# Mixture-of-experts stage on one core: weight fetches in two transfers and shorter runs, with the third, fourth and second expert and the last tiles placed anew

## The chip, the cores and the metric

One core of a Trainium2 chip runs the whole program. The metric is the device time in microseconds of one execution, so less is better. Times below are from one execution under the hardware profiler, counted from the start of its span, unless a median of runs is named.

## What is computed

Four residual blocks over x of 4 x 1024 rows of 256 channels, each behind a layer norm:

```python
x = x + attn0(layernorm(x))       # 16 heads, circulant projections
x = x + moe(layernorm(x))         # the stage that the change touches
x = x + attn1(layernorm(x))       # 16 heads with a position bias, gated output
x = x + ffn1(layernorm(x))        # 256 x 256 on fp8-rounded rows

# moe: 8 experts, top 2 of each row by a Sinkhorn plan pi, D = 256, F = 1024
g = jnp.einsum('nd,efd->enf', xf, W_gate)
u = jnp.einsum('nd,efd->enf', xf, W_up)
y = jnp.einsum('enf,edf->end', jax.nn.silu(g) * u, W_down)
out = out + y[top_idx[:, k], n_ar] * pi[:, k:k + 1]       # k = 0, 1
```

Everything is float32 at the surface. The kernel splits each float32 operand of a product into a rounded "high" part and the rest, "low", and adds three products (high x high, high x low, low x high).

## The kernel before, in words

The experts' stage (class Experts) runs from about 719 to 1453 us of the profile. The 8192 pairs of row and expert are sorted by expert into 71 tiles of 128 rows (MOE_TILES); the tiles of one expert follow one another, about nine each. `plan` is a small table in SBUF, filled at run time, which says for every tile which expert it belongs to, which experts come next (SECOND, THIRD, FOURTH), whether the tile is the first of a new expert (IS_NEW), and which of the two weight buffers it uses (BUFFER, OTHER_BUFFER). Whoever needs such a number reads it with `planned` (L2351: a load and two register instructions).

An expert's weights are 3 MB: gate, up and down, 8 KB each per partition. They are kept three times, as they came (e_w_raw) and as high and low parts (e_w_high, e_w_low), each with two buffers. ACT makes the high parts (`high_part`, `high_second`), DVE the low ones (`low_part`, `low_second`); `high_ready` and `low_ready` count the parts in a fixed order over the tiles, and a part is counted, by a drain, in tiles without a new expert too. When both are made of a raw buffer, it is free for the fetch of the expert after next but one.

For each tile j, on the engines:

- PE (`pe`): gate product, transposes of the next tile's rows, up product, then the down product of tile j-2 (LAG = 2). A gate and up product are 24 matmuls, a down product 24 shorter ones.
- ACT (`act`): `split_hidden(j-2)` (high part of the turned hidden rows, e_hT), SiLU of the gate product (e_hid), the conditional fetch of an expert (`fetch_fourth(j-2)`), `high_part` of gate and up, `move_y(j-2)` (e_y from PSUM), `high_part` of down.
- DVE (`dve`): `rest_of_hidden(j-2)` (low part of e_hT), `low_part` of down and of up, `split_rows(j+1)` (e_xT), the product of SiLU and up (e_hid), its 32 x 32 transposes (e_squares), `low_part` of gate.
- SP (`sync`): stores e_squares to DRAM (`store_squares`, 512 KB) and loads them back turned (`load_turned`, four transfers, runs of 1 KB). The last two tiles (BY_PE and on) are turned by PE instead (`turn_hidden`).
- POOL: gathers the rows of a tile, scatters its results.

The order is written out by hand; nothing schedules it. The first expert comes by SP in three transfers ahead of the stage; the second and the third (L2385) by SP too, right behind each other; the fourth by POOL, once `low_second` has released the second's raw buffer, which is in tile 1, 2 or 3 if the expert changes there and otherwise behind tile 3 (REST = 4). All later fetches are ACT's, 3 MB in one transfer in runs of 4 KB (WEIGHT_RUN), in the second tile after a change of expert; `cond` makes them no transfer in all other tiles. At a change, tile s, the next expert's gate and up are made high in tile s of ACT, its down in tile s+1, and low one after the other in DVE's tiles s, s+1 and s+2.

Of the kernel before, what the change touches and what calls it, by code (L numbers as in the profile page):

```python
# [2069 lines left out]
W_BUFS = 2  # L2070
WEIGHT_RUN = 4096
AHEAD = W_BUFS + 1
# [239 lines left out]
class Experts:  # L2312
# [3 lines left out]
    BY_PE = MOE_TILES - LAG  # L2316
    REST = 4
    Q, R = 4, 32
# [34 lines left out]
    def high_value(self, kind, j):  # L2353


        order = []
        for k in range(1, MOE_TILES):
            order += [("second", k)] * (k < self.REST) + [("up", k)] + [("down", k - 1)] * (k > 1)
            order += [("second", k + 1)] * (k + 1 == self.REST)
        return order.index((kind, j)) + 1  # L2360

    def low_value(self, kind, j):


        order = []
        for k in range(1, MOE_TILES):
            order += [("second", k)] * (k < self.REST) + [("down", k - self.LAG)] * (k > self.LAG)
            order += [("up", k - 1)] * (k > 1) + [("gate", k)]
            order += [("second", k + 1)] * (k + 1 == self.REST)
        order += [("up", MOE_TILES - 1), ("down", MOE_TILES - 2)]  # L2370
        return order.index((kind, j)) + 1
# [12 lines left out]
    def fetch(self, e, buf, row, j, sem):  # L2384
        e.dma_start(self.w.raw[:, buf, :],  # L2385
                    self.w.weights[bass.ds(self.planned(e, row, j), 1), :, :].rearrange("e p n -> p (e n)")
                    ).then_inc(sem, DMA)

    def sync(self, e, mirror_stored, beside):
        e.wait_ge(self.rows_in[1], DMA)  # L2390
        mirror_stored(e)
        self.fetch(e, 0, SECOND, 0, self.second_in)
        e.wait_ge(self.first_low, 3)
        beside(e, (2, 3))
        self.fetch(e, 1, THIRD, 0, self.weights_in)
        for j in range(self.BY_PE):
            self.store_squares(e, j)
            self.load_turned(e, j)
        e.wait_ge(self.second_in, DMA)
# [36 lines left out]
    def pool(self, e):  # L2436
        def fetch_fourth(k):
            with self.if_second(e, k):
                e.wait_ge(self.low_ready, self.low_value("second", k))
                self.fetch(e, 0, FOURTH, 0, self.fourth_in)  # L2440

        e.wait_ge(self.routed, 1)
        for j in range(ROW_BUFS):
            self.load_rows(e, j)
        e.wait_ge(self.routed, 2)
        for j in range(MOE_TILES):
            if 1 <= j < self.REST:
                fetch_fourth(j)
# [4 lines left out]
            if j + 1 == self.REST:  # L2453
                fetch_fourth(self.REST)
        for j in range(MOE_TILES - self.LAG, MOE_TILES):
            self.store_y(e, j)
        e.wait_ge(self.fourth_in, DMA)
        for o in range(Y_BUFS):
            e.wait_ge(self.y_out[o], DMA * ((MOE_TILES + Y_BUFS - 1 - o) // Y_BUFS))

    def act(self, e):
# [8 lines left out]

        def high_part(j, a, b):
            with e.If(self.planned(e, IS_NEW, j) > 0):
                e.wait_ge(self.weights_in, DMA * min(max(1, j - 1), MOE_TILES - 1 - self.LAG))
                if j >= 2:
                    e.wait_ge(self.fourth_in, DMA)
                high_of(bass.ds(self.planned(e, OTHER_BUFFER, j), 1), a, b)
            e.drain().then_inc(self.high_ready, 1)

        def fetch_fourth(j):
            e.wait_ge(self.low_ready, self.low_value("down", j))  # L2480
            e.dma_start(self.w.raw[:, bass.ds(self.planned(e, OTHER_BUFFER, j), 1), :],
                        self.w.weights[bass.ds(self.planned(e, FOURTH, j), 1), :, :].rearrange("e p n -> p e n"),
                        cond=self.planned(e, IS_NEW, j) > 0, max_dma_last_dim=WEIGHT_RUN).then_inc(self.weights_in, DMA)

# [7 lines left out]
        def split_hidden(j):  # L2492
            self.wait_turned(e, j)
            if j:
                e.wait_ge(self.downed, j)
            high, whole = self.parts_of_hidden(j, 0)
            e.activation(high, whole, ACT.Copy).then_inc(self.h_high, 1)  # L2497

        for j in range(MOE_TILES):
# [9 lines left out]
            e.activation(self.hid[:, :], self.GU[:, 0, :], ACT.Silu).then_inc(self.silu, 1)  # L2509
            if self.LAG < j < MOE_TILES - 1:  # L2510
                fetch_fourth(j - self.LAG)
            if j >= 1:
                e.wait_ge(self.upped, j)
                high_part(j, 0, DOWN_AT)
            if j >= self.LAG:
                move_y(j - self.LAG)
                high_part(j - 1, DOWN_AT, WIDE)
            if j + 1 == self.REST:
                high_second(self.REST)
        for j in range(self.BY_PE, MOE_TILES):  # L2520
            split_hidden(j)
            move_y(j)

    def wait_turned(self, e, j):
        if j < self.BY_PE:
            e.wait_ge(self.turned_in[j % 2], self.Q * DMA * (j // 2 + 1))
        else:
            e.wait_ge(self.h_turned, j - self.BY_PE + 1)

    def parts_of_hidden(self, j, part):  # L2530

        out = self.hT[:, part, :, :].bitcast(FP32R)
        if j >= self.BY_PE:
# [5 lines left out]
    def dve(self, e, beside):  # L2539
# [10 lines left out]
        def rest_of_hidden(j):  # L2550
            low, whole = self.parts_of_hidden(j, 1)
            high = self.hT[:, 0, :, :]
# [3 lines left out]
            if j:  # L2556
                e.wait_ge(self.downed, j)
            e.tensor_tensor(low, whole, high, ALU.subtract).then_inc(self.h_low, 1)  # L2558
# [44 lines left out]
        for j in range(MOE_TILES):  # L2603
# [13 lines left out]
            if j:  # L2617
# [5 lines left out]
        low_part(MOE_TILES - 1, "up", DC * F, DOWN_AT)  # L2623
        low_part(MOE_TILES - 2, "down", DOWN_AT, WIDE)
        for j in range(self.BY_PE, MOE_TILES):
            rest_of_hidden(j)

    def pe(self, e):
# [60 lines left out]
        def down(j):  # L2689
# [7 lines left out]
            for f in range(FC):  # L2697
                mm = product(j, self.Y, (self.hT[:, 0, f, :], self.hT[:, 1, f, :]), DOWN_AT + f * D, D, f == 0,
                             f == FC - 1)
# [4 lines left out]
        for j in range(MOE_TILES):  # L2704
# [736 lines left out]
```

## Time and profile before

| | |
|---|---|
| median of 3 runs | 2167.04 us (2166.58 to 2167.49) |
| profiled execution, its own time | 2164.73 us |
| its span | 2163.1 us |
| mean granted TensorE clock | 0.937 of full |
| experts' stage | 719 to 1453 us |
| busy in the span: PE, DVE, ACT, POOL | 89%, 62%, 64%, 33% |

A row of the timeline gives start and duration in us, engine, line, operation and tiles, and in brackets the idle time before it with what ended that. "issue" is time with no wait that the profile shows. ACTq, SPq and DVEq are the sequencers' own instructions. The chain of waits is followed back from the last instruction of the span or of a window. Of the DMA views, q1 is SP's queue, q10 is ACT's and q0 is POOL's.

### The profile page before, as it was taken

To read this page: it belongs to the slowest core of one execution; us is meant where nothing else is said; L and a number is where in the kernel's file an instruction comes from. 1 tells how busy PE (TensorE), PEld (TensorE's weight loads), DVE (VectorE), ACT (ScalarE), POOL (GpSimd) and SP (SyncE) were. 2 spreads that over 40 slices of the span, in tenths; PEclk is the share of its full clock that TensorE was granted. 3 is DMA by queue.
4 is the path that set the end of the run, shared out by engine and by line. 5 is a ranking of instruction groups with operands and counts; after the bars stand their busy time and mean duration, and the time that the engine had idled before them with its cause. 6 is when DMAs were issued, how large, how long until landed. Compare 5 with 4: busy or idle time off the path is not lost.

```text
span 2163.1 us, 37845 instructions
## 1 busy us (share of the span) xinstructions
PE 1915.4 (89%) x11671; PEld 1090.0 (50%) x11671; DVE 1331.6 (62%) x2221; ACT 1385.9 (64%) x1586; POOL 703.1 (33%) x697
## 2 busy tenths in 40 slices
PE   6999999999945579998998989976989999999998
PEld 5722333333332468887887878865722222222255
DVE  4511144445667545555465555427689999999967
ACT  5699999999832233233233233224799999999944
POOL 2000111111110212121222122111068888888932
PEclk9999999999955689999999999987999999999999
DMA  5744333444100644554544554529944426354021
GB/s 195 243 97 69 59 77 76 83 88 88 40 31 17 246 161 144 200 180 143 199 167 154 191 186 140 187 91 333 315 106 90 103 43 133 59 139 67 9 87 69
DMA packets 131072, 276.08 MB, mean 128 GB/s; under 512 B 18588, under 2 KB 69022, under 8 KB 129656
## 3 DMA queue, kind: packets, MB, share of 16 engines
q1 hardware_dynamic: 117160, 228.72, 38.2%
q10 hardware_dynamic: 6736, 22.94, 3.1%
q0 software_dynamic: 6960, 21.77, 3.0%
q8 instruction: 108, 1.77, 0.4%
q14 instruction: 108, 0.88, 0.1%
HBM read 365.58 MB, written 96.21 MB: 213 GB/s over the span
## 4 chain that ended last, share of the span: by engine, by line
PE 46%; ACT 21%; DVE 13%; DMA 7%; issue 7%; POOL 3%; DVEq 1%; ACTq 1%; SPq 1%; POOLq 0%
PE psum L2654 16%; PE psum L1345 12%; PE psum L1326 9%; ACT A1f_probs L1370 8%; ACT A1f_probs L1378 8%; DMA hidden<-e_squares 4%; PE psum L381 3%; DVE e_w_low L2575 2%; ACT e_w_high L2463 2%; DMA e_turned<-hidden 2%; POOL A1f_probs L1547 2%; PE psum L850 1%; DVE e_hT L2558 1%; PE psum L396 1%; ACTq L2351 1%
## 5 line engine op out<-in xcount | busy, mean ns | idle before, releaser
L1326 PE MATMUL psum<-A_qa,A_ka 50*128 50x512 f32 x2048 | 408.3, 467 | 23.5 <-DVE A_qa L1413 6.2
L1326 PEld LDWEIGHTS psum<-A_qa,A_ka 50*128 50x128 f32 x2048 | 176.4, 185 | 470.5 <-DVE A1f_probs L1423 243.4
L2654 PE MATMUL psum<-e_w_high,e_xT 128*128 x1136 | 389.5, 406 | 22.0 <-DVE e_xT L2548 20.2
L1547 POOL TENSOR_TENSOR A1f_probs<-A1f_probs,A1f_bias 128x512 f32<-128x512 f32 x256 | 327.1, 1288 | 81.4 <-ACT A1f_probs L1378 81.0
L1423 DVE SCALAR_TENSOR_TENSOR A1f_probs<-psum,A1f_bias 128x1024 f32<-128x1024 f32 x256 | 311.6, 1217 | 23.5 <-PE psum L1326 19.7
L1378 ACT ACTIVATE A0f_probs<-psum 128x1024 f32<-128x1024 f32 x256 | 315.5, 1232 | 0.0
L1366 ACT ACTIVATE A0f_probs<-psum 128x1024 f32<-128x1024 f32 x256 | 313.2, 1224 | 2.7 <-PE psum L1326 2.7
L2654 PE MATMUL psum<-e_w_high,e_hT 128*128 x1136 | 236.8, 301 | 59.6 <-DVE e_hT L2558 59.6
L1345 PE MATMUL psum<-A1f_probs,v 128*32 128x512 f32 x2048 | 274.0, 606 | 17.2 <-POOL A1f_probs L1547 16.2
L1370 ACT ACTIVATE A1f_probs<-A1f_probs 128x1024 f32<-128x1024 f32 x256 | 274.0, 1070 | 4.5 <-DVE A1f_probs L1423 3.5
L1345 PE MATMUL psum<-A0f_probs,v 128*32 128x512 f32 x2048 | 273.8, 607 | 0.0
L1378 ACT ACTIVATE A1f_probs<-psum 128x1024 f32<-128x1024 f32 x256 | 263.7, 1030 | 0.0
L2654 PEld LDWEIGHTS psum<-e_w_high,e_xT 128*128 128x128 f32 x1136 | 219.2, 193 | 67.9 <-issue 24.4
L2433 POOL DMA_INDIRECT results<-e_y,places x71 | 70.4, 992 | 549.0 <-ACT e_y L2490 539.3
L2490 ACT ACTIVATE e_y<-psum 128x256 f32<-128x256 f32 x71 | 27.2, 384 | 323.5 <-PE psum L2654 322.4
L2654 PEld LDWEIGHTS psum<-e_w_high,e_hT 128*128 128x128 f32 x1136 | 197.9, 208 | 69.5 <-issue 67.5
L2654 PE MATMUL psum<-e_w_low,e_xT 128*128 x568 | 225.8, 397 | 0.0
L2558 DVE TENSOR_TENSOR e_hT<-e_turned,e_hT 128x1024 fp32r<-128x1024 f32 x69 | 86.0, 1247 | 149.1 <-ACT e_hT L2497 145.2
L2654 PE MATMUL psum<-e_w_low,e_hT 128*128 x568 | 170.0, 299 | 0.0
L2497 ACT ACTIVATE e_hT<-e_turned 128x1024 fp32r<-128x1024 f32 x69 | 73.1, 1060 | 95.5 <-DMA e_turned<-hidden 65.9
L1431 DVE SCALAR_TENSOR_TENSOR psum<-A1f_bias,psum 128x512 f32<-128x512 f32 x195 | 133.5, 685 | 0.0
L2654 PEld LDWEIGHTS psum<-e_w_low,e_xT 128*128 128x128 f32 x568 | 110.5, 195 | 18.6
(297 smaller groups left out, 2506.3 us busy)
## 6 DMA issues: line engine op xcount, KB each, us to landing
e_w_raw<-in_experts ACTq DMA_DIRECT2D x67, 3072.0 KB
hidden<-e_squares SPq DMA_DIRECT2D x69, 512.0 KB
e_turned<-hidden SPq DMA_DIRECT2D x276, 128.0 KB
qk_parts<-L_part SPq DMA_DIRECT2D x64, 512.0 KB, 4.1
A_qa<-qk_parts SPq DMA_DIRECT2D x192, 128.0 KB, 4.2
A_ka<-qk_parts SPq DMA_DIRECT2D x192, 128.0 KB, 6.3
om<-results SPq DMA_DIRECT2D x16, 512.0 KB, 6.9
e_w_raw<-in_experts SPq DMA_DIRECT2D x2, 3072.0 KB
```

What stands on the lines that cost most here:

```text
L1326: mm = e.matmul(ps[:, side * HALF:(side + 1) * HALF], self.qk.ka[rows, s, pair, kt * P:(kt + 1) * P].bitcast(FP32R), self.qk.qa[rows, s, p ...
L1345: pv = e.matmul(O[32 * i:32 * (i + 1), :], self.v[:, b * BT + kt, h * VW:h * VW + 32], self.probs_of(n, i // PAIR)[:, side * HALF:(side + ...
L1366: e.activation(probs, self.buffer(w), ACT.Exp, scale=SCORE_SCALE).then_inc(self.exped[0], 1)
L1370: e.activation(probs, probs, ACT.Exp).then_inc(self.exped[0], 1)
L1378: e.activation(self.probs_of(n, 1), self.buffer(w), ACT.Exp, scale=SCORE_SCALE).then_inc(self.exped[1], 1)
L1423: e.scalar_tensor_tensor(out=self.probs_of(n, 0).rearrange("p (h q) -> p h q", h=PAIR), in0=self.buffer(w).rearrange("p (h q) -> p h q", h ...
L1431: e.scalar_tensor_tensor(out=third, in0=self.bias_of(*w[1:], slice(PAIR, PAIR + 1)).rearrange("p h q -> p (h q)"), scalar=1.0 / SCORE_SCAL ...
L1547: e.tensor_tensor(fourth, fourth, self.bias_of(*w[1:], slice(self.FOURTH, GH)).rearrange("p h q -> p (h q)"), ALU.mult).then_inc(self.mult ...
L2433: e.indirect_dma_start(out=self.y_dram, out_offset=bass.IndirectOffsetOnAxis(ap=self.places[:, j:j + 1], axis=0), in_=self.y[:, o, :], in_ ...
L2497: e.activation(high, whole, ACT.Copy).then_inc(self.h_high, 1)
L2558: e.tensor_tensor(low, whole, high, ALU.subtract).then_inc(self.h_low, 1)
L2654: mm = e.matmul(out, left[part].bitcast(FP32R), moving.bitcast(FP32R), start=start and i == 0, stop=stop and i == 2)
```

## The change

It does five things.

1. Every fetch but the first expert's goes in runs of 1 KB (WEIGHT_RUN).
2. ACT's fetch becomes two: gate and up (2 MB) one tile after the new expert's first (`fetch_part(j-1, "up")`), down (1 MB) two tiles after (`fetch_part(j-2, "down")`). Each waits until its own part has been made low. Both stand in every tile, as transfers that `cond` may leave out. The first is where the SiLU's side of `move_y` is, the second behind the down part's `high_part`.
3. The third expert is fetched by ACT, behind the SiLU of tile 0, and the fourth by ACT behind the SiLU of tile 2; POOL has no fetch left.
4. REST goes from 4 to 2: `high_second` and `low_second` run behind tile 1.
5. The last tiles: tile 69's turned rows are kept in the two buffers of e_turned, free by then, and split ahead of the work of tile 70; PE turns tile 70 ahead of the down product of 69. SP's first loads of the next stage, which reuse that space, wait until that product is done. Parts that only a change at the last tile would need are left out.

```diff
-WEIGHT_RUN = 4096
+WEIGHT_RUN = 1024
...
-    REST = 4
+    REST = 2
+    LAST = MOE_TILES - 1
...
     def sync(self, e, mirror_stored, beside):
...
         beside(e, (2, 3))
-        self.fetch(e, 1, THIRD, 0, self.weights_in)
...
-        e.wait_ge(self.h_low, self.BY_PE)
+        e.wait_ge(self.downed, self.BY_PE + 1)
...
-        def fetch_fourth(j):
-            e.wait_ge(self.low_ready, self.low_value("down", j))
+        def fetch_part(j, kind, a, b, landed):
+            e.wait_ge(self.low_ready, self.low_value(kind, j))
...
             e.activation(self.hid[:, :], self.GU[:, 0, :], ACT.Silu).then_inc(self.silu, 1)
-            if self.LAG < j < MOE_TILES - 1:
-                fetch_fourth(j - self.LAG)
-            if j >= 1:
+            if j == 0:
+                e.wait_ge(self.first_low, 3)
+                self.fetch(e, 1, THIRD, 0, self.weights_in)
+            if j == self.REST:
+                e.wait_ge(self.low_ready, self.low_value("second", self.REST))
+                self.fetch(e, 0, FOURTH, 0, self.fourth_in)
+            if 1 <= j < self.LAST:
                 e.wait_ge(self.upped, j)
-                high_part(j, 0, DOWN_AT)
+                high_part(j, "up", 0, DOWN_AT)
+            if 1 < j < self.LAST - 1:
+                fetch_part(j - 1, "up", 0, DOWN_AT, self.weights_in)
+            if j == self.LAST:
+                split_hidden(self.BY_PE)
             if j >= self.LAG:
                 move_y(j - self.LAG)
-                high_part(j - 1, DOWN_AT, WIDE)
+                high_part(j - 1, "down", DOWN_AT, WIDE)
+            if self.LAG < j < self.LAST:
+                fetch_part(j - self.LAG, "down", DOWN_AT, WIDE, self.second_in)
...
+            if j == self.LAST:
+                rest_of_hidden(self.BY_PE)
             multiply(j)
...
-        down(MOE_TILES - self.LAG)
-        turn_hidden(MOE_TILES - 1)
-        down(MOE_TILES - 1)
+        turn_hidden(self.LAST)
+        down(self.BY_PE)
+        down(self.LAST)
```

ACT between `move_y` (e_y) and the next `split_hidden` (e_hT), in any middle tile. Before, from the down part's `high_part` on:

```order
L2463 ACTIVATE e_w_high<-e_w_raw 128x2048
L2472 UNCONDITIONAL_BRANCH
L2497 ACTIVATE e_hT<-e_turned 128x4x8x32
L2509 ACTIVATE e_hid<-psum 128x1024
L2351 TENSOR_LOAD plan
```

The change, from the same instruction on:

```order
L2455 ACTIVATE e_w_high<-e_w_raw 128x2048
L2464 UNCONDITIONAL_BRANCH
L2352 TENSOR_LOAD plan
L2352 ISA x2
L2352 TENSOR_LOAD plan
L2352 ISA x2
L2352 TENSOR_LOAD plan
L2352 ISA x2
L2476 ISA x2
L2476 DMA e_w_raw<-in_experts 128x8x256
L2494 ACTIVATE e_hT<-e_turned 128x4x8x32
```

A fetch with its three readings of the plan now stands between the two, in every tile.

ACT in tile 70. Before, behind that tile's last high part:

```order
L2497 ACTIVATE e_hT<-psum 128x1024 [waits e_downed,e_h_turned]
L2490 ACTIVATE e_y<-psum 128x256 [waits e_y_out0,e_downed]
L2497 ACTIVATE e_hT<-psum 128x1024 [waits e_downed,e_h_turned]
L2490 ACTIVATE e_y<-psum 128x256 [waits e_y_out1,e_downed]
L3273 ACT_TABLE_LOAD [waits met]
```

The change, from the SiLU of tile 70 on:

```order
L2506 ACTIVATE e_hid<-psum 128x1024 [waits e_hidden,e_gated]
L2494 ACTIVATE e_turned<-psum 128x1024 [waits e_h_low,e_h_turned]
L2485 ACTIVATE e_y<-psum 128x256 [waits e_y_out2,e_downed]
...
L2494 ACTIVATE e_hT<-psum 128x1024 [waits e_downed,e_h_turned]
L2485 ACTIVATE e_y<-psum 128x256 [waits e_y_out0,e_downed]
L2485 ACTIVATE e_y<-psum 128x256 [waits e_y_out1,e_downed]
```

Tile 69's split has moved ahead of the e_y of tile 68 and no longer waits for a down product; only tile 70's does, for that of tile 68.

## Rows read from the trace of the kernel before

**Rows 1.** The page: busy time of each engine and its share of the span.
```profile
PE 1915.4 (89%) x11671; PEld 1090.0 (50%) x11671; DVE 1331.6 (62%) x2221; ACT 1385.9 (64%) x1586; POOL 703.1 (33%) x697
```

**Rows 2.** Chain of waits, start and length in us: the beginning, then two middle tiles.
```profile
731.81 16.18 DMA hidden<-e_squares
...
777.42 6.56 DVE e_w_low L2575
...
987.00 8.38 PE psum L2654 x48
995.60 8.39 PE psum L2654 x48
```

**Rows 3.** Timeline, PE: idle ahead of the down products of tiles 0 and 2.
```profile
755.19 0.58 PE L2654 MATMUL psum<-e_w_high,e_hT 128*128 x1 [14.63 <-DVE e_hT L2558]
...
785.53 0.58 PE L2654 MATMUL psum<-e_w_high,e_hT 128*128 x1 [9.60 <-DVE e_hT L2558]
```

**Rows 4.** Timeline, all engines, one middle tile.
```profile
931.18 0.38 ACT L2490 ACTIVATE e_y<-psum 128x256 f32<-128x256 f32 x1 [4.82 <-PE psum L2654]
...
932.02 1.06 ACT L2497 ACTIVATE e_hT<-e_turned 128x1024 fp32r<-128x1024 f32 x1 [0.46 <-issue]
...
933.12 1.26 DVE L2558 TENSOR_TENSOR e_hT<-e_turned,e_hT 128x1024 fp32r<-128x1024 f32 x1 [2.24 <-ACT e_hT L2497]
...
936.71 0.28 PE L2654 MATMUL psum<-e_w_high,e_hT 128*128 x1
```

**Rows 5.** Timeline, DVE, around the change of expert at 1175.
```profile
1170.77 1.27 DVE L2558 TENSOR_TENSOR e_hT<-e_turned,e_hT 128x1024 fp32r<-128x1024 f32 x1 [2.23 <-ACT e_hT L2497]
1173.15 0.42 DVE L2546 CAST e_xT<-psum 128x256 fp32r<-128x256 f32 x1 [1.11 <-issue]
...
1182.55 1.22 DVE L2558 TENSOR_TENSOR e_hT<-e_turned,e_hT 128x1024 fp32r<-128x1024 f32 x1 [0.19 <-issue]
1185.39 2.29 DVE L2575 TENSOR_TENSOR e_w_low<-e_w_raw,e_w_high  x1 [1.61 <-issue]
```

**Rows 6.** Timeline, ACT, around the same change.
```profile
1168.84 0.38 ACT L2490 ACTIVATE e_y<-psum 128x256 f32<-128x256 f32 x1 [4.84 <-PE psum L2654]
...
1175.60 3.63 ACT L2463 ACTIVATE e_w_high<-e_w_raw  x1 [2.98 <-issue]
...
1188.41 1.91 ACT L2463 ACTIVATE e_w_high<-e_w_raw  x1 [0.94 <-issue]
1190.48 1.06 ACT L2497 ACTIVATE e_hT<-e_turned 128x1024 fp32r<-128x1024 f32 x1 [0.15 <-issue]
...
1223.17 0.38 ACT L2490 ACTIVATE e_y<-psum 128x256 f32<-128x256 f32 x1 [6.01 <-PE psum L2654]
```

**Rows 7.** Timeline, SP: a store and the load behind it, with no fetch beside them.
```profile
1168.57 0.34 SPq L2409 DMA_DIRECT2D hidden<-e_squares  x1
1171.18 1.73 SPq L2419 DMA_DIRECT2D e_turned<-hidden  x4
```

**Rows 8.** Chain of waits: the store that goes beside a fetch.
```profile
1200.19 9.12 DMA hidden<-e_squares
```

**Rows 9.** DMA queues: q1 in 1172 to 1176 (1 KB runs), q10 in 1197 to 1212.
```profile
q1 hardware_dynamic: 576, 0.52, 41.8%
...
q10 hardware_dynamic: 784, 3.15, 60.2%
```

**Rows 10.** Timeline, ACT: e_y of tiles 5, 67 and 70.
```profile
818.29 0.38 ACT L2490 ACTIVATE e_y<-psum 128x256 f32<-128x256 f32 x1 [4.82 <-PE psum L2654]
...
1426.56 0.38 ACT L2490 ACTIVATE e_y<-psum 128x256 f32<-128x256 f32 x1 [4.84 <-PE psum L2654]
...
1452.84 0.38 ACT L2490 ACTIVATE e_y<-psum 128x256 f32<-128x256 f32 x1 [6.05 <-PE psum L2654]
```

**Rows 11.** Windows, 1216 to 1223: the granted clock is the third number from the end.
```profile
1216.00:1223.00 7.00, 5.35 (x25) 5.36 (x26) 4.45 (x5) 1.16 (x2) 0.00 (x0) 0.53 0.30 92
```

**Rows 12.** Timeline, PE: the down product of tile 69.
```profile
1439.06 0.58 PE L2654 MATMUL psum<-e_w_high,e_hT 128*128 x1 [3.29 <-DVE e_hT L2558]
```

More of the change, by code:

```diff
@@ L2357, in high_value @@
         for k in range(1, MOE_TILES):
-            order += [("second", k)] * (k < self.REST) + [("up", k)] + [("down", k - 1)] * (k > 1)
+            order += [("second", k)] * (k < self.REST) + [("up", k)] * (k < self.LAST)
+            order += [("down", k - 1)] * (k > 1)
             order += [("second", k + 1)] * (k + 1 == self.REST)
@@ L2367, in low_value @@
             order += [("second", k)] * (k < self.REST) + [("down", k - self.LAG)] * (k > self.LAG)
-            order += [("up", k - 1)] * (k > 1) + [("gate", k)]
+            order += [("up", k - 1)] * (k > 1) + [("gate", k)] * (k < self.LAST)
             order += [("second", k + 1)] * (k + 1 == self.REST)
-        order += [("up", MOE_TILES - 1), ("down", MOE_TILES - 2)]
+        order += [("down", self.LAST - 1)]
         return order.index((kind, j)) + 1
@@ L2436, in pool @@
     def pool(self, e):
[L2437 to L2440, printed above, removed]
         e.wait_ge(self.routed, 1)
@@ L2469, in high_second, with high_part @@
             e.drain().then_inc(self.high_ready, 1)
-        def high_part(j, a, b):
+        def high_part(j, kind, a, b):
             with e.If(self.planned(e, IS_NEW, j) > 0):
-                e.wait_ge(self.weights_in, DMA * min(max(1, j - 1), MOE_TILES - 1 - self.LAG))
-                if j >= 2:
-                    e.wait_ge(self.fourth_in, DMA)
+                if kind == "down":
+                    e.wait_ge(self.second_in, DMA * min(max(1, j - 1), MOE_TILES - 1 - self.LAG))
+                else:
+                    e.wait_ge(self.weights_in, DMA * min(max(1, j - 1), MOE_TILES - 1 - self.LAG))
+                    if j >= 2:
+                        e.wait_ge(self.fourth_in, DMA)
                 high_of(bass.ds(self.planned(e, OTHER_BUFFER, j), 1), a, b)
             e.drain().then_inc(self.high_ready, 1)
-        def fetch_fourth(j):
-            e.wait_ge(self.low_ready, self.low_value("down", j))
-            e.dma_start(self.w.raw[:, bass.ds(self.planned(e, OTHER_BUFFER, j), 1), :],
-                        self.w.weights[bass.ds(self.planned(e, FOURTH, j), 1), :, :].rearrange("e p n -> p e n"),
-                        cond=self.planned(e, IS_NEW, j) > 0, max_dma_last_dim=WEIGHT_RUN).then_inc(self.weights_in, DMA)
+        def fetch_part(j, kind, a, b, landed):
+            e.wait_ge(self.low_ready, self.low_value(kind, j))
+            e.dma_start(self.w.raw[:, bass.ds(self.planned(e, OTHER_BUFFER, j), 1), a:b],
+                        self.w.weights[bass.ds(self.planned(e, FOURTH, j), 1), :, a:b].rearrange("e p n -> p e n"),
+                        cond=self.planned(e, IS_NEW, j) > 0, max_dma_last_dim=WEIGHT_RUN).then_inc(landed, DMA)
         def move_y(j):
@@ L2528, in wait_turned, with hT_free, hT_of @@
             e.wait_ge(self.h_turned, j - self.BY_PE + 1)
+    def hT_free(self, j):
+        return self.BY_PE if j == self.LAST else j
+    def hT_of(self, j, part):
+        return self.turned[:, part, :].rearrange("p (f n) -> p f n", f=FC) if j == self.BY_PE else self.hT[:, part, :, :]
     def parts_of_hidden(self, j, part):
-        out = self.hT[:, part, :, :].bitcast(FP32R)
+        out = self.hT_of(j, part).bitcast(FP32R)
         if j >= self.BY_PE:
@@ L2551, in rest_of_hidden @@
             low, whole = self.parts_of_hidden(j, 1)
-            high = self.hT[:, 0, :, :]
+            high = self.hT_of(j, 0)
             high = high.rearrange("p f n -> p (f n)") if j >= self.BY_PE else high.rearrange(
@@ L2555, in rest_of_hidden @@
             e.wait_ge(self.h_high, j + 1)
-            if j:
-                e.wait_ge(self.downed, j)
+            if j and j != self.BY_PE:
+                e.wait_ge(self.downed, self.hT_free(j))
             e.tensor_tensor(low, whole, high, ALU.subtract).then_inc(self.h_low, 1)
@@ L2622, in dve @@
                 next(beside, None)
[L2623 to L2626, printed above, removed]
+        low_part(self.LAST - 1, "down", DOWN_AT, WIDE)
+        rest_of_hidden(self.LAST)
     def pe(self, e):
```

22 lines of the change are left out of this document (10 added, 12 removed).

## The prediction

> **What bounds the kernel now.** I read the page first: PE is busy for 89% of the span and no other engine for more than 64% [rows 1], so what isn't PE's work shows up as idle PE. In the chain of waits a middle tile takes 995.60 - 987.00 = 8.60 us, all of it PE [rows 2]; 71 tiles would be 611 us, and the stage takes some 734. Three places hold the rest.
>
> The beginning: PE idles 14.63 us before down product 0 and 9.60 before down product 2 [rows 3]. The first is the store of tile 0, which lands 16.18 us after its issue, behind the second and third expert on SP's queue; the second is the second expert's conversion, its low part alone 6.56 us, at a time when nothing else waits [rows 2].
>
> The seven changes of expert: from the e_y of tile 5 to that of tile 67 are 608.3 us [rows 10], 62 tiles at 8.60 are 533.2, so a change loses 10.7 us. At the one I followed, five tiles take 1223.17 - 1168.84 = 54.3 us, a loss of 11.3 [rows 6]. Half of that is order: DVE turns to e_hT only behind its low part [rows 5]. The other half is the DMA: a store lands in 2.6 us by itself [rows 7] and in 9.12 beside the fetch [rows 8]; PE then waits, and its clock is granted at 0.53 of full, so for nearly all of these 7 us at 1.2 GHz, the lower level [rows 11].
>
> The end: PE idles 3.29 us before down product 69 [rows 12], since e_hT is one buffer and each split waits for the product before.
>
> **The change, part by part.**
>
> *Beginning.* The third expert leaves SP's queue, so the store of tile 0 shares the engines with it in place of standing behind it. Ahead of it are the second expert and two 0.5 MB loads. It landed at 748.0 [rows 2]; by bytes (about 4.7 MB ahead and in turn with the third's) I take 743.5, between 740 (the third gets no share) and 748 (all bytes must go first). The second expert's high part (REST = 2) is made while PE waits for that store anyway. DVE then does its squares of tile 1 and the low part: some 2.2 us from the squares' start to the low part, 6.56 for it [rows 2], 1.24 for e_hT, so down product 0 starts at 753.8, 1.4 earlier. Then nothing is left to convert: tiles follow at PE's pace, down product 2 at 772.9 instead of 785.53 [rows 3]. The fourth expert's transfer (ACT at about 753) now falls on the store of tile 2, priced at 1.5 us. Behind that the old kernel still loses 2 us to its fourth fetch and 2 to the lower clock, until e_y of tile 5 at 818.29 [rows 10]. Together -15 us; bounds -17 and -9.
>
> The Trainium skill (DMA: Bandwidth & Descriptors, Issuing engines are not separate DMA queues) says that transfers of all issuers run on the same 16 engines and interleave, so that spreading them saves only issue time. By that rule the store still lands at 748, and this term is -11, not -15.
>
> *Every middle tile.* Between e_y and e_hT on ACT there are 0.84 us now (931.18 to 932.02) [rows 4]. One fetch costs ACT's sequencer 2.98 - 0.94 = 2.04 us even when it moves nothing: the gap before the high part with a fetch ahead of it, less the gap without [rows 6]. The fetch that stays is moved behind the high part of gate and up and costs the same there; the new one lengthens the 0.84 to 2.9. PE needs e_hT 936.71 - 931.18 = 5.53 us after e_y [rows 4]; it gets it after 2.9 + 1.10 + 1.26 + 0.14 = 5.4. So it is just in time. The second limit is the round through both engines, since the fetch of gate and up waits for DVE's count: 2.9 (e_y to e_hT), 1.1 (to DVE's), 2.38 from there to the e_xT cast, ahead of which the count is given [rows 5], 2.04 for the fetch: 8.4 to 8.5 us against PE's 8.60. Cover of 0.1 us in some 50 tiles: I cost it at nothing for most and 0.3 us for one in five, +3; bounds 0 and +25. If the cover goes, each tile pays in full.
>
> *Each change of expert*, timed like the one at 1175 [rows 5, 6]. ACT: e_y at 1168.8, e_hT 1171.8, SiLU, high part of gate and up 1174.1 to 1177.7 (1.5 earlier, as no fetch is ahead of it), fetch, e_y at 1180.0, fetch, e_hT at 1182.9. DVE's e_hT runs from 1184.0 (1182.55 before), its low part of up ends 2.84 + 2.29 later, at 1189.1. ACT's transfer of gate and up waits for exactly this, and e_y, the high part of down (1.32 later, 1.91 long) and the next e_hT are queued behind it: e_y at 1191.6, high part to 1194.9, fetch, e_hT at 1197.1 instead of 1190.48. DVE's low part of down ends at 1202.4; the next fetch on ACT waits for the count behind it (1203.2); e_y 1205.4, the 1 MB transfer, e_hT 1208.7, and one round later e_hT at 1217.2. Down product on PE at 1219.7, its e_y at 1222.6: where the old kernel was (1223.17). So the DMA's wait goes, and waits of ACT for DVE take its place. Against the average change (10.7 and not 11.3) this is +0.2; PE's four gaps, 1.7 to 2.9 us each, let its clock fall once more, +1.1. Seven times 1.3 is +9; bounds -5 (the DVE counts come 2 us sooner than I place them) and +25.
>
> The transfers themselves: a 1 KB run takes 0.418 x 4 x 16 / 576 = 0.046 us of an engine (four in 0.186), a 4 KB run 0.602 x 15 x 16 / 784 = 0.184 beside other traffic [rows 9]. 2 MB are 128 runs per engine, 5.9 us, and no tile waits for them, as the next expert is used some 70 us later. What matters is how long a store waits beside one: I take 1 us, near the 2.6 of the store alone [rows 7], since the 4 KB pieces of a store go in turn with 1 KB ones; the other bound is the 6.5 more of [rows 8].
>
> The Trainium skill (same page, Queues, rings and completion order) has an engine serve up to about 17 descriptors of one ring before the next. With 17 runs of 0.184 us a store waits 3 us for each turn, with 17 of 0.046 less than 1; by the first figure the sum would be some 15 us more over seven changes, by the second it stays.
>
> *POOL* loses its one fetch and waits for nothing: no change. *SP's* first loads for the next stage start at 1439.9 instead of 1429.8; they are 3.6 us of issue and are needed after 1450: hidden, and at most +3 if not.
>
> *End.* Tile 69 is split while PE runs the up product of 70, so its down product follows that of 68 at 1437.0 (1439.06 before [rows 12]) and at full clock; tile 70 is turned in front of it, its split waits only for product 68: 1437.2 + 1.06 + 1.24, covered by product 69. Down product 70 at 1440.5, its e_y at 1443.5 against 1452.84 [rows 10]: -9.3; bounds -10 and -6.
>
> *Sum:* -15 + 3 + 9 - 9.3 = -12 on the profiled execution's own 2164.73 us (span 2163.1): 2152.7. The median of the runs is 2.3 above that execution; I carry the difference over: 2155.
>
> **The rivals.**
>
> 1. *The gains at both ends stand and changes cost as forecast* (my forecast): 2155, own range 2146 to 2164. Chance 0.50.
> 2. *The store isn't sooner, as all run on the same engines*: 2159, by the term above. For it: a store issued behind nothing on its own queue still took 9.12 us beside another queue's fetch [rows 8]. Against: the third's bytes needn't all precede the store's. 0.13.
> 3. *The beginning's wait moves instead of going*: the fourth fetch delays the stores of tiles 2 and 3 by 6.5 us each, as beside a fetch now [rows 8], and the gain is 5 or less: 2165, no difference. 0.14.
> 4. *Slower: ACT becomes the bound of every tile.* The place is the new fetch between e_y and e_hT, the price what the round exceeds 8.60 by; it decides from 0.1 us on. With 0.45 us more in 50 tiles: 2155 + 23 = 2178. For it: cover of 0.1 us [rows 4], 2.04 us added to an engine that reads the plan seven times a tile. Against: the sum of measured steps is still below. 0.15.
> 5. *The waits for counts overlap more than I see*, and a change keeps only its first loss, some 5.4: 2155 - 9 - 37 = 2109, or half of it. For it: half of each loss was the DMA. Against: the program's order. 0.08.
>
> **How the numbers follow.** The time is the likeliest case's, 2155. The range leaves out case 5 and half of case 4: 2138 to 2176. Two tenths of a per cent, 4.3 us, is about what a measurement of this kernel can tell from no change. Faster by more: nearly all of 1, most of 2, all of 5: 0.65. Within: parts of 1 and 2, most of 3: 0.17. Slower: 4 and a little of 3: 0.18.
>
> **What would show it.** PE's idle time before down product 2 gone, the 6144-wide conversion at about 738; e_y of tile 5 near 802. In a middle tile e_y to e_hT of 2.9 us with PE still at 8.60 a tile; 8.9 or more is rival 4. At a change, no 9 us store, an ACT fetch that waits for a low part, the e_hT after next some 6 us later, and 10 to 13 us lost; 5 or 6 would be rival 5. The last e_y some 3.6 us after that of tile 69 and 17 after that of 67. I am wrong if tiles lengthen, or if DMA landings still end PE's waits.

## The result: slower by 1.4%, and the profile after

| | before | changed |
|---|---|---|
| median of 4 runs | 2167.26 us (2166.58 to 2174.42) | 2199.22 us (2196.41 to 2200.51) |
| profiled execution's span | 2163.1 | 2198.7 |
| mean granted TensorE clock | 0.937 | 0.944 |

The ratio is 1.0138, 95% interval 1.0115 to 1.0162. The forecast was 2155 with a range to 2176. The page's busy times against [rows 1]: PE is busy 10 us longer, DVE and ACT are busy no longer than before, and the span is 36 us longer.

```profile
PE 1925.1 (88%) x11671; PEld 1080.3 (49%) x11671; DVE 1325.9 (60%) x2221; ACT 1379.8 (63%) x1586; POOL 703.8 (32%) x696
```

Timeline, ACT, of the changed kernel: e_y of tiles 5, 67 and 70, as in [rows 10].

```profile
808.86 0.39 ACT L2485 ACTIVATE e_y<-psum 128x256 f32<-128x256 f32 x1 [4.41 <-PE psum L2669]
...
1466.65 0.39 ACT L2485 ACTIVATE e_y<-psum 128x256 f32<-128x256 f32 x1 [4.31 <-PE psum L2669]
...
1483.66 0.38 ACT L2485 ACTIVATE e_y<-psum 128x256 f32<-128x256 f32 x1 [3.41 <-PE psum L2669]
```

The stage's first fetch, of the first expert, is issued by SP ahead of anything that the edits touch. Timeline, SP, before and changed:

```profile
700.14 2.70 SPq L2097 DMA_DIRECT2D e_w_raw<-in_experts  x3
```
```profile
702.71 2.70 SPq L2097 DMA_DIRECT2D e_w_raw<-in_experts  x3
```

These rows, SP's first load of results behind the stage (1458.38 and 1491.20) and the span cut the difference into six:

| stretch | before | changed | difference | forecast |
|---|---|---|---|---|
| to the first fetch | 700.1 | 702.7 | +2.6 | 0 |
| from there to e_y 5 | 118.2 | 106.1 | -12.0 | -15 |
| e_y 5 to e_y 67 | 608.3 | 657.8 | +49.5 | +3 + 9 |
| e_y 67 to e_y 70 | 26.3 | 17.0 | -9.3 | -9.3 |
| e_y 70 to SP's first load | 5.5 | 7.5 | +2.0 | 0 |
| behind that | 704.7 | 707.5 | +2.8 | 0 |

The first and the last stretch are not the change's: in the fourteen profiled executions below, the first fetch comes between 696.5 and 702.7 us, whatever the edits, and the last stretch takes 704.7 to 708.6 us, 708.5 in a kernel whose last tiles are as before. Of the rest, the two ends gave 21.3 us and the 62 tiles between took back more than twice that. A middle tile is no longer 8.60 us. Timeline of one, other engines' rows left out:

```profile
1076.66 0.38 ACT L2485 ACTIVATE e_y<-psum 128x256 f32<-128x256 f32 x1 [3.65 <-PE psum L2669]
...
1079.93 1.06 ACT L2494 ACTIVATE e_hT<-e_turned 128x1024 fp32r<-128x1024 f32 x1 [2.90 <-issue]
...
1081.03 1.23 DVE L2573 TENSOR_TENSOR e_hT<-e_turned,e_hT 128x1024 fp32r<-128x1024 f32 x1 [3.28 <-ACT e_hT L2494]
...
1083.07 0.28 PE L2669 MATMUL psum<-e_w_high,e_hT 128*128 x1
...
1085.22 0.10 ACTq L2476 DMA_DIRECT2D e_w_raw<-in_experts  x1
...
1086.14 0.39 ACT L2485 ACTIVATE e_y<-psum 128x256 f32<-128x256 f32 x1 [4.23 <-PE psum L2669]
```

From e_y to e_y are 9.48 us. From e_y to e_hT are 3.27 (forecast 2.9, before 0.84 [rows 4]), to the end of DVE's part 5.60 (1081.03 + 1.23 - 1076.66). The fetch of gate and up leaves at 1085.22, 0.92 before the next e_y. And the chain of waits in the same place shows something that [rows 2] never had in a middle tile, 0.61, 0.13 and 0.70 us of "issue" between the down product (x24, or the end of x36) and the next gate product (x12). Where a gap is long, the next tile's down product is late by it; where it is short, ACT is late again in the tile after:

```profile
1071.03 1.07 ACT e_hT L2494
1072.12 1.24 DVE e_hT L2573
1073.36 0.13 issue
1073.49 3.13 PE psum L2669 x24
1076.62 0.61 issue
1077.23 3.02 PE psum L2669 x12
...
1086.11 0.13 issue
...
1089.47 5.80 PE psum L2669 x36
1095.27 0.70 issue
```

A change of expert, the one that [rows 6] show for before, now on ACT, with the two low parts on DVE:

```profile
1190.58 0.38 ACT L2485 ACTIVATE e_y<-psum 128x256 f32<-128x256 f32 x1 [4.17 <-PE psum L2669]
...
1201.80 0.39 ACT L2485 ACTIVATE e_y<-psum 128x256 f32<-128x256 f32 x1 [2.26 <-issue]
...
1213.92 0.38 ACT L2485 ACTIVATE e_y<-psum 128x256 f32<-128x256 f32 x1 [6.78 <-issue]
...
1228.61 0.39 ACT L2485 ACTIVATE e_y<-psum 128x256 f32<-128x256 f32 x1 [6.32 <-issue]
```
```profile
1209.09 2.29 DVE L2590 TENSOR_TENSOR e_w_low<-e_w_raw,e_w_high  x1 [1.60 <-issue]
...
1222.89 2.29 DVE L2590 TENSOR_TENSOR e_w_low<-e_w_raw,e_w_high  x1 [0.26 <-issue]
```

The three steps are 11.2, 12.1 and 14.7 us; the forecast had 11.2, 11.6 and 13.8. The two tiles behind take 9.5 us each (forecast 8.6), so the five take 57.1 us, where the forecast had 53.8 and the kernel before 54.3. Twice e_y comes only 2.5 and 3.4 us behind the end of a low part, with a fetch between: ACT waits for DVE's count, as forecast. SP's queue shows that a store beside the 2 MB fetch still takes 8.6 us (1214.89 to 1223.46), but nobody waits for it here:

```profile
1214.89 0.34 SPq L2410 DMA_DIRECT2D hidden<-e_squares  x1
1223.46 1.73 SPq L2420 DMA_DIRECT2D e_turned<-hidden  x4
```

### The profile page after: what moved, and what is told of

Read it like the earlier page. It is cut to its first block, busy times and chain, and to the rows that moved or that the text cites. A ratio compares the mean times of both kernels' runs of the same rounds, so it can differ in the third digit from the quotient of the medians.

```text
span 2198.7 us, 38602 instructions
## 1 busy us (share of the span) xinstructions
PE 1925.1 (88%) x11671; PEld 1080.3 (49%) x11671; DVE 1325.9 (60%) x2221; ACT 1379.8 (63%) x1586; POOL 703.8 (32%) x696
## 4 chain that ended last, share of the span: by engine, by line
PE 42%; ACT 21%; DVE 13%; issue 9%; ACTq 5%; DMA 4%; POOL 3%; DVEq 2%; SPq 1%; POOLq 0%
PE psum L2669 15%; PE psum L1345 12%; PE psum L1326 9%; ACT A1f_probs L1370 8%; ACT A1f_probs L1378 8%; ACTq L2352 4%; DVE e_w_low L2590 2%; PE psum L381 2%; ACT e_hT L2494 2%; DMA qk_parts<-L_part 2%; POOL A1f_probs L1547 1%; PE psum L850 1%; DVEq L2352 1%; DVE e_hT L2573 1%; ACTq L2476 1%
## 5 line engine op out<-in xcount | busy, mean ns | idle before, releaser
L2669 PE MATMUL psum<-e_w_high,e_xT 128*128 x1136 | 397.3, 413 | 50.4 <-DVE e_xT L2563 25.7
L1423 DVE SCALAR_TENSOR_TENSOR A1f_probs<-psum,A1f_bias 128x1024 f32<-128x1024 f32 x256 | 311.7, 1217 | 24.6 <-PE psum L1326 21.3
L1366 ACT ACTIVATE A0f_probs<-psum 128x1024 f32<-128x1024 f32 x256 | 313.1, 1223 | 3.0 <-PE psum L1326 3.0
L2669 PE MATMUL psum<-e_w_high,e_hT 128*128 x1120 | 225.4, 294 | 48.8 <-DVE e_hT L2573 47.9
L2434 POOL DMA_INDIRECT results<-e_y,places x71 | 75.7, 1067 | 593.5 <-ACT e_y L2485 579.5
L2669 PEld LDWEIGHTS psum<-e_w_high,e_hT 128*128 128x128 f32 x1120 | 186.6, 199 | 66.6 <-issue 65.3
L2669 PE MATMUL psum<-e_w_low,e_hT 128*128 x560 | 162.8, 291 | 0.0
```

Of the source, the lines that this page charges most:

```text
L1366: e.activation(probs, self.buffer(w), ACT.Exp, scale=SCORE_SCALE).then_inc(self.exped[0], 1)
L1423: e.scalar_tensor_tensor(out=self.probs_of(n, 0).rearrange("p (h q) -> p h q", h=PAIR), in0=self.buffer(w).rearrange("p (h q) -> p h q", h ...
L2669: mm = e.matmul(out, left[part].bitcast(FP32R), moving.bitcast(FP32R), start=start and i == 0, stop=stop and i == 2)
```

## The experiments

Twelve kernels ran. "Middle tile" below is the median step from e_y to e_y over the 27 steps from tile 6 to 67 that lie away from changes; "per change" is what the other 35 steps, five from each change on, take over 8.60 us apiece, divided by seven (so it holds slow tiles among these five, and none behind them). "To e_y 5" counts from the stage's first fetch, since that itself moves by 6 us from execution to execution. All these are from the profiled execution; the ratio is to runs of the kernel before that were made beside each kernel's own.

| kernel | median us | ratio, 95% interval | to e_y 5 | 5 to 67 | middle tile | per change |
|---|---|---|---|---|---|---|
| before | 2167.26 to 2169.00 | | 118.2 | 608.3 | 8.60 | 10.6 |
| changed | 2199.22 | 1.0138 (1.0115 to 1.0162) | 106.1 | 657.8 | 9.47 | 14.4 |
| up early | 2164.76 | 0.9973 (0.9957 to 0.9988) | 106.0 | 631.0 | 9.52 | 10.6 |
| down early | 2166.73 | 0.9997 (0.9982 to 1.0013) | 103.7 | 631.1 | 8.86 | 13.6 |
| both early | 2137.54 | 0.9868 (0.9833 to 0.9902) | 103.0 | 601.9 | 8.61 | 9.0 |
| plan read once | 2125.69 | 0.9811 (0.9776 to 0.9847) | 102.8 | 589.4 | 8.61 | 7.3 |
| one fetch | 2140.55 | 0.9865 (0.9848 to 0.9882) | 102.8 | 604.3 | 8.61 | 9.9 |
| short runs only | 2168.04 | 0.9987 (0.9969 to 1.0005) | 117.6 | 607.9 | 8.59 | 10.6 |
| start only | 2157.27 | 0.9953 (0.9937 to 0.9970) | 107.6 | 609.8 | 8.61 | 10.8 |
| end only | 2162.12 | 0.9974 (0.9955 to 0.9993) | 118.4 | 611.7 | 8.59 | 11.1 |
| four reads | 2236.09 | 1.0303 (1.0273 to 1.0333) | 121.5 | 680.0 | 9.43 | 17.8 |
| two reads | 2188.70 | 1.0088 (1.0059 to 1.0116) | 120.0 | 635.6 | 8.75 | 13.7 |
| PE reads ahead | 2184.67 | 1.0068 (1.0049 to 1.0087) | 104.4 | 643.4 | 9.01 | 13.7 |
| read once + PE | 2128.18 | 0.9820 (0.9782 to 0.9859) | 102.9 | 583.7 | 8.61 | 7.2 |

### Where the two fetches stand

Three kernels move one or both fetches of the changed kernel to where the old one was, behind the SiLU, for tile j-2 (where the fetch of down is moved, the wait of down's `high_part` counts one landing more, since that fetch now stands ahead of it).

```diff
+            if self.LAG < j < self.LAST:
+                fetch_part(j - self.LAG, "up", 0, DOWN_AT, self.weights_in)
             if 1 <= j < self.LAST:
                 e.wait_ge(self.upped, j)
                 high_part(j, "up", 0, DOWN_AT)
-            if 1 < j < self.LAST - 1:
-                fetch_part(j - 1, "up", 0, DOWN_AT, self.weights_in)
```

That is "up early". "Down early" puts the unchanged fetch of down in the same place, and "both early" does both.

> The changed kernel, but ACT's fetch of gate and up belongs to the tile before (j-2) and stands behind the SiLU, ahead of the high part, as the old fetch did; what it waits for is long done. The fetch of down stays between e_y and e_hT. Theory A (the round through ACT, DVE's count for the up part, the fetch behind it and e_y sets the tile: 3.5 + 1.1 + 2.2 + 2.5 + 0.1 = 9.4 us in the changed kernel's trace): without the wait for the count a middle tile is back at 8.6 us, e_y to e_hT still 3.0 to 3.5, and the time 2150 to 2160. Theory B (PE gets e_hT late whatever ACT waits for: 3.5 + 1.1 + 1.2 + 0.1 = 5.9 us behind e_y where PE needs it at 5.5, and PE's queue then starts the gate product late): middle tiles stay at 9.0 to 9.5 and the time is 2175 to 2200. Theory C (neither place matters, the transfers do): 2195 to 2200.

> The changed kernel, but the fetch of down stands behind the SiLU, ahead of the high part of gate and up; the fetch of gate and up stays behind that part and still waits for DVE's count. Theories A and B: e_y to e_hT is 0.84 us again, the round 0.84 + 1.1 + 2.2 + 2.5 = 6.6, middle tiles 8.60 us, the time near 2150 (2199 less about 30 in middle tiles and about 20 at the changes of expert). Theory C: 2195 to 2200, tiles 9.5.

> The changed kernel, but both fetches stand one behind the other behind the SiLU, ahead of the high part, and belong to tile j-2. ACT then spends 4.1 to 4.7 us on fetches where it had 2.9 us of slack before e_y beside the old fetch's 2.06, so 0.3 to 0.9 us is left. Theories A and B: middle tiles 8.60 us, time 2145 to 2160; a change of expert loses no wait for a low count, so it may be 3 to 5 us cheaper than in the kernel with only down early. If ACT's slack is used up, tiles of 8.7 to 9.0 and 2165 to 2175. Theory C: 2195 to 2200.

C falls: the same transfers leave in all four kernels. A and B each hold half, and the times missed every range: 2164.76 lies between those of A and B, down early (2166.73, expected near 2150) saves less and both early (2137.54) more than expected. With "up" early no fetch waits for a fresh count, and middle tiles stay at 9.5 us all the same: not the round (A) but the lateness of e_hT (B) decides there. Its chain of waits has the same loop, from the stretch between e_y and e_hT over both e_hT and the down product to 0.67 us of issue:

```profile
1062.32 1.07 ACT e_hT L2494
1063.41 1.24 DVE e_hT L2573
1064.64 0.13 issue
1064.78 3.12 PE psum L2669 x24
1067.90 0.67 issue
1068.57 3.02 PE psum L2669 x12
```

The fetch of gate and up waiting for its count costs at the changes: 14.4 to 10.6 us each, 7 x 3.8 = 27 us, which is all that this kernel gains in the stretch. With "down" early it is the other way round: e_y to e_hT falls to 0.85 to 1.5 us, the changes keep 13.6, and middle tiles fall to a median of 8.86. That they are not all at 8.60 is a round through both engines after all, but not that of theory A: e_y's idle time is ended by DVE's count (L2603), not by PE, and it is the moved fetch of down that waits for it. DVE gives the count of down right behind its part of e_hT, 3.8 us behind e_y (1055.87), and then both fetches, one on either side of the high part, hold ACT for 5.1 us:

```profile
1060.97 0.39 ACT L2485 ACTIVATE e_y<-psum 128x256 f32<-128x256 f32 x1 [5.49 <-DVEq L2603]
```

Each edit takes 27 us from the stretch by itself and 29 when the other is made too (657.8, 631.0, 631.1, 601.9): two costs that add up, and between them the whole +49.5 and 6 us more. Both early beats the kernel before.

Both early and the one-fetch kernel below differ in one thing, whether the transfer is split in two, at the same place and for the same tile: 2137.54 and 2140.55 us, with intervals that overlap, and 9.0 against 9.9 us per change. So the split by itself is worth little.

### The plan read once

```diff
         def fetch_part(j, kind, a, b, landed):
+            if j not in read:
+                read[j] = [self.planned(e, row, j) for row in (OTHER_BUFFER, FOURTH, IS_NEW)]
+            buf, expert, is_new = read[j]
             e.wait_ge(self.low_ready, self.low_value(kind, j))
```

> The changed kernel, both fetches in its places, but the three numbers of the plan are read once per tile, ahead of the wait for the count, and the fetch of down takes them from registers. Theories A and B: e_y to e_hT falls from 3.5 to about 1.6 us, the fetch of gate and up behind the count from 2.5 to about 0.6, the round to about 5.7: middle tiles 8.60 us; at a change ACT still waits for DVE's low part of up, so changes stay dearer than before: 2150 to 2165. Theory C: 2195 to 2200.

2125.69 us, 24 below the expected range and the fastest; one other can't be told from it. Both fetches and the wait stay where the change put them, only the reads go: the stretch between e_y and e_hT is 1.35 us in middle tiles, and these are at 8.61. The changes cost 7.3 us each, less than in any kernel with the old single fetch. So placing the transfers as the change does is no mistake. What it pays for is the reads: of the 2.7 us that the fetch of down had put between e_y and e_hT (a median of 3.54 against 0.84) they are 2.2, and 0.5 stays.

### The parts alone

One fetch: the changed kernel with the old single transfer of 3 MB at its old place. Short runs:

```diff
-WEIGHT_RUN = 4096
+WEIGHT_RUN = 1024
...
-                    ).then_inc(sem, DMA)
+                    max_dma_last_dim=WEIGHT_RUN).then_inc(sem, DMA)
```

Start only: the kernel before with REST = 2, the third expert's fetch taken from SP and POOL's `fetch_fourth` taken out, and on ACT, behind the SiLU,

```diff
+            if j == 0:
+                e.wait_ge(self.first_low, 3)
+                self.fetch(e, 1, THIRD, 0, self.weights_in)
+            if j == self.REST:
+                e.wait_ge(self.low_ready, self.low_value("second", self.REST))
+                self.fetch(e, 0, FOURTH, 0, self.fourth_in)
```

End only: the kernel before with everything of the diff that speaks of LAST, BY_PE, `hT_free` and `hT_of`.

> The changed kernel, but ACT's fetch is one transfer of 3 MB again, where the kernel before has it; runs of 1 KB, both ends and the placing of experts two to four as changed. Middle tiles 8.60 us. Theory D (runs of 1 KB are what frees the stores beside a fetch): a change of expert loses only its first part, 5 to 7 us instead of 10.7, and the time is 2168 - 12 (start) - 5 (end) - 30 = about 2120. Theory E (the split into two transfers at different tiles is what frees them): a change still loses 10 to 11 us and the time is 2148 to 2152.

> The kernel before with one edit: every fetch goes in runs of 1 KB. Theory D: a store issued beside a fetch lands in 3 to 4 us instead of 9.12 and the seven changes lose 5 to 7 us each: 2135 to 2150. Theory E: the same bytes pass the same engines, a store still lands in 8 to 9 us, the time is 2165 to 2172.

> The kernel before with only the placing of the experts changed: the third by ACT behind tile 0's SiLU, the fourth by ACT in tile 2, REST = 2; long runs as before, except that the third and fourth keep their 24 KB pieces. Theory F (placing alone gives the start): e_y of tile 5 near 806 instead of 818.3 and 2154 to 2158. Theory G (without the 1 KB runs the stores of tiles 0, 2 and 3 stand behind long runs): e_y of tile 5 at 813 to 818, 2163 to 2168.

> The kernel before with only the last tiles changed, SP's later wait among it. Theory H (the late loads of the next stage cost what the changed kernel loses behind its last e_y, 4.3 us): the last e_y 9.2 us sooner against that of tile 67, but the whole only 4 to 6 us faster: 2162 to 2164. Theory I (those 4.3 us have another source): 9 us faster, 2159 to 2160.

Short runs by themselves are worth nothing that was measured (POOL's fetch of the fourth expert goes in 4 KB pieces there, not 1 KB), and the store beside a fetch takes 9.03 us, against 9.12 in [rows 8]; its chain of waits:

```profile
1202.39 9.03 DMA hidden<-e_squares
```

Over all seven changes that store takes 8.5 to 10.5 us from its issue to the load behind it before, and 7.5 to 9.9 with short runs, 9.1 and 8.4 on the mean; the next tile's store goes from 4.6 to 5.8. The trace's packets say where the time goes. Of a store alone the first packet starts 0.84 us behind the issue, beside a fetch 3.6 to 3.9 us behind it with runs of 4 KB and 3.7 to 4.4 with runs of 1 KB. Only the stretch from its first packet to its last gets shorter, from 4.6 to 3.7 us on the mean. What holds the first packet back is open.

In the one-fetch kernel these stores take 6.9 to 9.2 us and a change still costs 9.9, so D falls. E falls too where it says that the split frees the stores: with it they still take 8.6 us in the changed kernel and 6.3 to 8.3 with both early. The one-fetch kernel's 2140.55 us is 7.5 below E's range: its start gives 15.4 us and not 12, and its 62 tiles 4.0.

Start only gives 10.6 us by e_y 5 and 10 in the whole, which is F, a little short. With runs of 1 KB as well (one fetch) e_y 5 comes 15.4 sooner than before, and short runs alone make it 0.6. The two help each other, and the store of tile 0 shows how. Counted from the stage's first fetch it lands after 47.9 us before, 48.2 with start only and 48.1 with short runs only, but after 44.1 in the one-fetch kernel. So the third expert's fetch delays it as much from ACT's queue as from SP's, as long as it goes in its 24 KB pieces; it takes both edits to bring the store forward by 4 us.

End only: e_y 67 to 70 falls to 16.8 us, and the whole gains 5.6, in H's range. Behind the last e_y 3.1 us are lost, but H's cause for it is not shown. SP's first load of results starts 7.89 us behind the last e_y, where it was 5.54 (1452.84 to 1458.38):

```profile
1443.95 0.38 ACT L2491 ACTIVATE e_y<-psum 128x256 f32<-128x256 f32 x1 [3.41 <-PE psum L2667]
...
1451.84 4.05 SPq L310 DMA_DIRECT2D om<-results  x8
```

These 2.4 us lie in POOL's wait for the landing of the last scatter. The wait ends 4.8 us behind that scatter's issue and not 2.4, the drain behind it takes 2.27 us in both, and then all engines go on. Whether the late loads or the last three scatters, now 3.8 us apart, delay that landing was not separated. The other 0.8 us lie in the later stages, whose length moves by more than that between the kernels.

### Lateness by itself, and PE's sequencer

Two kernels add nothing to the kernel before but reads of the plan on ACT (four or two), no transfer and no wait. Two more let PE read its two numbers for the next tile ahead of the wait for e_hT.

```diff
                 high_part(j - 1, DOWN_AT, WIDE)
+            if 3 <= j < MOE_TILES - 1:
+                for _ in range(4):
+                    self.planned(e, IS_NEW, j)
```

On the changed kernel, for PE:

```diff
             if j >= self.LAG:
+                if j + 1 < MOE_TILES:
+                    is_new(j + 1), buffer_of(j + 1)
                 down(j - self.LAG)
```

> The kernel before with one addition: ACT reads the plan four times, for nothing, between the high part of down and the next e_hT in every middle tile; no transfer and no wait is added. It measures late e_hT by itself: e_y to e_hT becomes 0.84 + 4 x 0.53 = 2.9 us or a little more. Theory J (PE wants e_hT only where its down product starts, 5.53 us after e_y): 2.9 + 2.5 = 5.4 is in time, tiles stay at 8.60 and the time at 2168 to 2172. Theory K (PE's sequencer, which stands at the wait for e_hT, must be let through some 0.7 us sooner, or its reads of the plan ahead of the next gate product show): middle tiles of 9.1 to 9.6, the time 2185 to 2205.

> As the run with four reads, but with two: e_y to e_hT 0.84 + 1.06 = 1.9 us. Theories J and K both: in time (4.4 us), tiles 8.60, 2167 to 2170. If tiles lengthen here too, what PE needs lies earlier than either says.

> The changed kernel, but PE reads the two numbers of the plan for the next tile ahead of its wait for e_hT; nothing else moves, the branch stays where it is. Theory K: about 1.0 of the 1.8 us that PE's sequencer takes between a down and a gate product is done while it waits, the gap of 0.6 to 0.7 us ahead of the gate product is gone, middle tiles are 8.8 to 9.0 us instead of 9.5, and the time is 2199 - 20 to 30, 2168 to 2180. Theory J: the gap has another source and the time stays at 2195 to 2200.

> Reads of the plan once in ACT and ahead of the wait on PE, both together. Middle tiles are 8.60 us in the kernel with ACT's reads alone, so only the late tiles around a change of expert can gain: three or four of 9.5 us each, 0.65 us apiece, seven times. Theory K: 2126 - 10 to 15, 2110 to 2118. Theory J: 2124 to 2128.

Four reads make middle tiles of 9.43 us, as slow as the changed kernel's, and 2236 us, 30 more than K's upper end, since the five tiles around a change lengthen too (17.8 against 10.6). The gap is there, 0.61 and 0.68 us of issue ahead of a gate product:

```profile
1096.56 3.13 PE psum L2657 x24
1099.69 0.61 issue
1100.30 3.02 PE psum L2657 x12
...
1118.56 0.68 issue
```

J can't explain these gaps. It isn't refuted by the tiles' length, since e_y to the end of DVE's e_hT became 6.0 us on the median and not the expected 5.4, late by J too. Two reads cost 20 us, which neither theory expected, and put numbers on the limit. In 13 of its 27 middle tiles DVE's part of e_hT ends 4.21 to 4.56 us behind e_y, and PE doesn't idle before the next gate product. At 4.65 to 5.07 it does, for 0.04 to 0.28 us (12 tiles; one at 4.66 has none, its down product being late itself), at 5.21 for 0.57. In the kernel before it is at 3.20. So the limit is about 4.6, where I had put it at 5.4 (5.53 less 0.14).

With PE's reads ahead of the wait, the changed kernel's gap falls to 0.11 us, a middle tile from 9.47 to 9.01 and the time by 14.6 us:

```profile
1089.08 1.24 DVE e_hT L2573
1090.32 0.14 issue
1090.45 5.88 PE psum L2669 x36
...
1099.33 0.11 issue
```

So the 0.87 us that a middle tile lost are in two halves. 0.46 go with PE's reads. Its sequencer's rows in the changed kernel show why they cost: let through at 1073.36, it hands out the down product until 1075.3 and then takes 1.8 us for two reads and a branch, until 1077.12, while the product is over at 1076.62. Let through earlier, it is ahead of the engine: in the kernel before it starts on these reads at 1077.24, with 2.4 us of the down product still to run. The other 0.41 are plain lateness: 5.84 us from e_y to the down product and 3.17 from there to the next e_y (medians), where the kernel before has 5.53 and 3.07. That is J's mechanism, and it holds for this half. The time was 5 us above K's range. Added to the plan read once, the same edit gives no measurable difference (2128.18 against 2125.69, both with some 10 us between their runs), though the profiled stretch is 5.7 us shorter, nearly all of it in late tiles that had reached past the five behind a change; I expected 10 to 15.

## Why the prediction was wrong, point by point

**Every middle tile: this step failed.** It was costed at +3, with +25 as a bound; measured are 0.87 us in each of the 27 tiles away from changes, +23, and more at the changes. The mechanism was rival 4's and it decided: but two terms of the sum "2.9 + 1.10 + 1.26 + 0.14 = 5.4, needed at 5.53" were off. The 2.9 was 3.0 to 4.1 (median 3.5), because reads of the plan at that place took up to 1.0 us and not 0.28. The engine also reads the plan eight times a tile now, not seven, and did so five times before. The 5.53 was read as the time at which PE starts the down product; the two-reads run shows that PE must be let through the wait by 4.6, since its sequencer does the next tile's reads behind that wait. Even the forecast's own 2.9, which makes 5.2, would have been late. "Cover of 0.1 us" should have been the warning: the price from there on is 0.9 us in each tile, so rival 4 had to be the likeliest, and its size 0.9 us and not 0.45. The second limit of the forecast, the round with cover of 0.1 us, was too low by the same reads (9.4 us for its 8.4 to 8.5), but did not decide: without it (up early) middle tiles stay at 9.52.

**Each change: right in mechanism, too cheap.** The waits for the counts came at the places named and as long as said, within 0.9 us per step. That the one of gate and up costs 27 us in all is shown by the kernel with "up" early. A change costs 14.4 us on the average and not the 12 of the forecast. The forecast set them against a gain from the DMA that it took for certain; and the late tiles behind each change, 0.9 us apiece, were missing, from the same mis-sized term.

**The store beside a fetch: wrong, and hidden.** I took 1 us for its delay with runs of 1 KB; the changed kernel's store takes 8.6, the short-runs kernel's 9.03. By the rule that I quoted from the Trainium skill (DMA: Bandwidth & Descriptors, Queues, rings and completion order), runs a quarter as long should have cut the wait to a third or less; beside the 3 MB fetches the trace does not agree (9.1 to 8.4 us on the mean), since some 3 us of the delay pass before the store's first packet, whatever the runs. In the changed kernel the delay cost nothing at the change followed, because ACT was later still.

**Beginning: right once the tiles are right.** -15 forecast; counted from the stage's first fetch, -12.0 measured, and -15.4 in the one-fetch kernel and with the plan read once: the missing part is in tiles 1 to 5, which take 46.5 us and not 43.1. The store of tile 0 lands 4.0 us sooner on that count (forecast 4.5), after 11.79 us instead of 16.18, and down product 0 starts 1.0 us sooner (forecast 1.4). So rival 2 falls here, and with it the rule of the Trainium skill (DMA: Bandwidth & Descriptors, Issuing engines are not separate DMA queues) as I had turned it into a time; but with start only, where the pieces stay at 24 KB, the store isn't sooner, as rival 2 has it. The number was right by luck in part: the forecast had it from the fetch's leaving SP's queue alone, and it takes the short runs too. Rival 3's mechanism is there: the store of tile 2, beside the fourth fetch, takes 6.8 us instead of 2.6, 4.2 more where I had 1.5 and the rival 6.5, and that of tile 1 5.9 instead of 4.0. It costs PE next to nothing, 0.32 us of idle time before down product 2.

```profile
734.78 11.79 DMA hidden<-e_squares
```

**End: right**, -9.3 between e_y 67 and e_y 70. Behind it, costed at nothing with +3 as a bound for **SP's late loads**, SP's first load of results comes 2.0 us later than before in the changed kernel and 2.4 in the end-only one. No run shows that the late loads are the cause.

**Rival 5**, changes that lose half, is what the plan read once comes near to: 7.3 us.

## What to carry to other kernels

A conditional transfer that moves nothing is not free: here it costs its engine's sequencer 2 us per tile, three quarters of it for reading its operands, and where that lies between an engine's last result and the next one a neighbour waits for, every iteration pays it. Read its operands once, early, ahead of waits, and keep them in registers. When the cover of a moved step comes out smaller than what was left out of the sum (here 0.1 us, in some 50 tiles), treat it as gone, and ask when the waiting engine's sequencer must pass the wait, not when its data path starts. And count stretches from a row inside the stage that no edit touches: here the start of the stage alone moved by 6 us between executions.

## What the hardware did that I had not expected

PE's sequencer works ahead only if its wait is met ahead. Met 2.3 us before the down product started (before), its reads for the next tile don't show. In the changed kernel's 27 middle tiles, met 0.9 us before or earlier, PE then idles for 0 to 0.10 us; met 0.74 to 0.82 before (one is the tile at 1076), for 0.13 to 0.28; met as the product starts, for 0.58 to 0.81. A read of the plan by ACT, 0.28 us as a rule, took 0.5 to 1.0 in many tiles; why is open. And shortening the runs of a 3 MB transfer from 4 KB to 1 KB hardly shortened the 512 KB store issued beside it (9.12 and 9.03 us in the two rows shown), since its first packet starts some 4 us behind the issue either way.
